# Edge stage opening: one semaphore per tile for the first four record loads, and the loads of super-tiles 1 to 4 each placed behind a gather

## The reference

```python
xs = x[:, :C] @ (W_in2f_s / np.sqrt(C))
xv = jnp.einsum('nci,cf->nfi', x[:, C:].reshape(n, C, 3), W_in2f_v) / np.sqrt(C)
sj = xs[idx_j]
vj = xv[idx_j]
...
h = shifted_softplus(f_ij @ Wf1 + bf1)
W = (h @ Wf2 + bf2) * rcut_ij[:, None]
m_s = s2 * W[:, :2 * F]
m_v = (v2.reshape(e, 2 * F, 3) * W[:, 2 * F:4 * F, None]).reshape(e, 6 * F)
...
agg = jax.ops.segment_sum(x_ij, idx_i, num_segments=n)
```

## Time and profile before

| what | value |
|---|---|
| median of three runs | 1488.72 us |
| profiled execution | 1492.38 us |
| its span | 1490.6 us |
| TensorE busy | 1352.1 us, 91% of the span |
| first record load of the edge stage issued | 442.17 us into the span |
| first gather | 446.04 us |
| last idle time of TensorE for a record load | ends at 463.40 us |
| last gather of the edge stage | 946.0 us |

### The profile page before, as it was taken

How to read it: one execution, slowest core, us unless ns; L and a number is a source line. 1 busy time by engine, 2 the same in 40 slices (tenths; PEclk the granted TensorE clock), 3 DMA queues, 4 the chain that set the end, 5 groups by cost and what they waited for, 6 DMA issues and landing times.

```text
span 1490.6 us, 28549 instructions
## 1 busy us (share of the span) xinstructions
PE 1352.1 (91%) x8675; PEld 610.0 (41%) x8676; DVE 987.0 (66%) x2481; ACT 625.1 (42%) x1097; POOL 753.2 (51%) x772
## 2 busy tenths in 40 slices
PE   6567998778879999999999999875999999999997
PEld 4244444435533333333333333462333343433333
DVE  7846666567737777777777777765564556556554
ACT  5455555554535666666666666571101111111110
POOL 4777777777767666666656666505312211211121
PEclk9667999989889999999999999996999999999999
DMA  5665333333239888888888888572351651524513
GB/s 200 227 216 165 111 115 113 113 115 115 101 111 311 257 257 256 256 256 256 256 248 267 255 257 257 187 282 61 65 192 29 197 183 28 197 82 136 191 29 95
DMA packets 125876, 262.54 MB, mean 176 GB/s; under 512 B 21073, under 2 KB 64808, under 8 KB 125147
## 3 DMA queue, kind: packets, MB, share of 16 engines
q0 software_dynamic: 48416, 141.37, 31.5%
q1 hardware_dynamic: 77410, 120.57, 24.5%
HBM read 204.35 MB, written 63.66 MB: 180 GB/s over the span
## 4 chain that ended last, share of the span: by engine, by line
PE 61%; POOL 22%; issue 8%; DVE 4%; DMA 4%; ACT 1%; SPq 0%; POOLq 0%; DVEq 0%; ACTq 0%
POOL edge_list L456 20%; PE psum L1378 18%; PE psum L1873 17%; PE psum L1885 8%; PE psum L1392 7%; PE psum L1387 5%; PE psum L1371 3%; POOL slot_list L1805 1%; DMA edge_list<-rec,place 1%; DMA out_x<-out_sums 1%; PE psum L1880 1%; DMA shared<-edge_list 1%; DMA slot_list<-pair,slots 1%; PE psum L1491 0%; PE psum L1576 0%
## 5 line engine op out<-in xcount | busy, mean ns | idle before, releaser
L1263 POOL DMA_INDIRECT shared<-node_table,shared x328 | 310.2, 946 | 196.3 <-DVE msg L1344 105.8
L456 POOL DMA_INDIRECT edge_list<-rec,place x313 | 316.9, 1013 | 97.4 <-issue 94.8
L1346 DVE TENSOR_TENSOR msg<-shared,psum 128x768 f32<-128x768 f32 x328 | 310.8, 948 | 0.0
L1378 PE MATMUL psum<-wf,hT 128*32 128x512 f32 x2624 | 298.2, 595 | 1.1 <-ACT hT L1295 0.7
L1873 PE MATMUL psum<-shared,zT 128*64 128x512 f32 (+1 forms) x960 | 295.7, 597 | 1.8 <-DVE zT L1991 1.5
L1301 ACT COPY psum<-bias 128x512 f32<-128x512 f32 x328 | 193.4, 590 | 175.8 <-DVE msg L1346 159.0
L1344 DVE TENSOR_TENSOR msg<-shared,psum 128x256 f32<-128x256 f32 x328 | 136.8, 417 | 120.1 <-PE psum L1378 119.2
L1873 PEld LDWEIGHTS psum<-shared,zT 128*64 128x64 f32 (+1 forms) x960 | 114.5, 159 | 180.7 <-issue 178.6
L1833 POOL DMA_DIRECT2D ids<-slot_list x20 | 11.5, 577 | 291.3 <-DVE zN L1960 266.7
L1885 PE MATMUL psum<-shared,hidT 128*64 128x512 f32 (+1 forms) x480 | 152.8, 597 | 2.8 <-DVE hidT L2012 2.8
L1378 PEld LDWEIGHTS psum<-wf,hT 128*32 128x32 f32 x2624 | 85.1, 110 | 163.4 <-issue 134.1
(11 more groups left out here) (355 smaller groups left out, 1517.8 us busy)
## 6 DMA issues: line engine op xcount, KB each, us to landing
shared<-edge_list SPq DMA_DIRECT2D x332, 130.0 KB
shared<-in_L_ffn_w_gate SPq DMA_DIRECT2D x8, 2048.0 KB, 9.3
shared<-in_L_ffn_w_up SPq DMA_DIRECT2D x8, 2048.0 KB, 14.8
shared<-in_L_ffn_w_down SPq DMA_DIRECT2D x8, 2048.0 KB, 19.6
shared<-node_table,shared POOLq DMA_INDIRECT x328
edge_list<-rec,place POOLq DMA_INDIRECT x313, 2.7
raw<-in_records SPq DMA_DIRECT2D x19, 256.0 KB, 3.8
xrow<-in_x SPq DMA_DIRECT2D x10, 250.0 KB
```

Of the source, the lines that this page charges most:

```text
L456: nc.gpsimd.indirect_dma_start(out=edge_list, out_offset=bass.IndirectOffsetOnAxis(ap=place[:n_, c:c + 1].bitcast(U32), axis=0), in_=rec[: ...
L1263: nc.gpsimd.indirect_dma_start(out=gat[:, k % G, :], out_offset=None, in_=table, in_offset=bass.IndirectOffsetOnAxis(ap=ix, axis=0)).then_ ...
L1346: nc.vector.tensor_tensor(m[:, 1:7, :].rearrange("p (a i) f -> p a i f", a=2), g[:, P:D].rearrange("p (i f) -> p i f", i=3).unsqueeze(1).t ...
L1378: ins = nc.tensor.matmul(WP[k % TS][q * W:(q + 1) * W, :], hT[:, (k // TS) % 2, at:at + W], wf2[:], start=False, stop=True, skip_group_che ...
```

## The change

Four semaphores `first_in[0..3]` are added for the four tiles of super-tile 0. Each of its first loads adds to its own semaphore, and each of the first four gathers waits for its own tile alone. TensorE, before it turns super-tile 0, waits for all four. SP no longer issues the loads of super-tiles 1 and 2 right behind those of super-tile 0: it loads super-tile 1 after gather 0 has landed, super-tile 2 after gather 2, super-tile 3 after gather 4, and super-tile 4 after gather 6.

`records_loaded0` is from now on used only from the second load into slot 0, so that the counts waited for on it are less by one load. The four new semaphores are used again as the first four of `z_out` in the node stage, with 16 more in each count. The number of semaphores stays the same, and so does the data that is moved.

```diff
+                first_in = [sem(f"first_tile{j}_then_z_out{j}") for j in range(TS)]
...
-                        for u in range(3):
-                            fetch(u, ahead[u])
-                        for k in range(LEAD):
-                            sp.wait_ge(gathered[k], 16)
-                        for u in range(3, NU - 1):
-                            fetch(u, ahead[u])
+                        for j in range(TS):
+                            sp.dma_start(er[:, 0, j, :], edge_list[bass.ds(ahead[0][j] * P, P), :]).then_inc(first_in[j], 16)
+                        sp.wait_ge(gathered[0], 16)
+                        fetch(1, ahead[1])
+                        sp.wait_ge(gathered[2], 16)
+                        fetch(2, ahead[2])
+                        sp.wait_ge(gathered[4], 16)
+                        fetch(3, ahead[3])
+                        sp.wait_ge(gathered[6], 16)
+                        fetch(4, ahead[4])
...
                         for k in range(G - 1):
-                            if k % TS == 0:
+                            if k < TS:
+                                pool.wait_ge(first_in[k], 16)
+                            elif k % TS == 0:
                                 pool.wait_ge(rec_in[k // TS], 16 * TS)
                             gather(k)
...
-                            pe.wait_ge(rec_in[u], landed)
+                            if landed is None:
+                                for j in range(TS):
+                                    pe.wait_ge(first_in[j], 16)
+                            else:
+                                pe.wait_ge(rec_in[u], landed)
...
-                        turn_hidden(0, 0, 16 * TS)
+                        turn_hidden(0, 0, None)
...
-                z_out = [z_out] + [sem(f"z_out{i}") for i in range(1, ZB)]
+                z_out = first_in + [z_out]
+
+                def rows_out(u, n_):
+                    return 16 * n_ + (16 if u < TS else 0)
```

More of the change, by code:

```diff
@@ L1273, in gather_ahead @@
                                 if k7 % TS == 0:
-                                    wait_alone(pool, rec_in[(k7 // TS) % NU], it * (16 * TS) + 16 * TS * (1 + k7 // NS))
+                                    u7 = (k7 // TS) % NU
+                                    wait_alone(pool, rec_in[u7], it * (16 * TS) + 16 * TS * ((u7 > 0) + k7 // NS))
                                 wait_alone(pool, made, it * (2 * NS) + (2 * k + 1))
@@ L1426, in super_tiles @@
                                     if u % 2 and (not last or u + d < nu):
-                                        turn_hidden((u + d) % NU, st + d, it * (16 * TS) + 16 * TS * (1 + (u + d) // NU))
+                                        turn_hidden((u + d) % NU, st + d, it * (16 * TS) + 16 * TS * (((u + d) % NU > 0) + (u + d) // NU))
                                 sums(u, st)
@@ L1450, in _ @@
                     for u in range(NU):
-                        wait_alone(sp, rec_in[u], n * (16 * TS) + (16 * TS if u < NU - 1 else 0))
+                        wait_alone(sp, rec_in[u], n * (16 * TS) + (16 * TS if 0 < u < NU - 1 else 0))
                     for k in range(G):
@@ L1557, in _ @@
                         for u in range(ZB):
-                            sp.wait_ge(z_out[u], 16 * len(range(u, NC_, ZB)))
+                            sp.wait_ge(z_out[u], rows_out(u, len(range(u, NC_, ZB))))
                     @block.tensor
@@ L1625, in normalise @@
                             if c >= ZB:
-                                act.wait_ge(z_out[c % ZB], 16 * (c // ZB))
+                                act.wait_ge(z_out[c % ZB], rows_out(c % ZB, c // ZB))
                             nc.scalar.activation(z_at[c % ZB][:CR, :], xrow[:CR, c, :], ACT.Identity, scale=rstd[:CR, c:c + 1],
@@ L1820, in _ @@
                     for u in range(ZB):
-                        pool.wait_ge(z_out[u], 16 * len(range(u, NC_, ZB)))
+                        pool.wait_ge(z_out[u], rows_out(u, len(range(u, NC_, ZB))))
                     pool.wait_ge(ids_found, 1)
```

2 lines of the change are left out of this document (1 added, 1 removed).

## The result

The changed kernel is slower: 1495.53 us in the median of seven runs (1491.63 to 1498.27), against 1489.39 of the kernel before on the same chip (1487.23 to 1496.05); ratio 1.0039, 95% interval 1.0026 to 1.0053. A second series gave 1.0052, 1.0033 to 1.0072. The forecast was 1.5 us more and the result is 5.8 to 7.7 us (the two ratios of 1489): 1495.53 lies above the forecast range of 1488.1 to 1493.2. A loss that can be told had a chance of 22% in the prediction.

The account below looks back on a forecast made before the run. TensorE was taken to bound the edge stage from super-tile 4's turn on; super-tile 2 turned 2.79 us later, less 1.31 us of waits, gives 1.48 us more: 1488.72 becomes 1490.2 us. The range was 1488.1 to 1493.2.

Parts of the forecast that it names:

- A loss that can be told: Whole kernel: slower by more than 0.2%, 3.0 us; chance 22%, against 74% same and 4% faster.
- the 1.31 us of waits comes off if they go: TensorE's waits between the turns of super-tiles 2 and 4 vanish, cutting the 2.79 us delay to 1.48.
- both waits are covered, by TensorE's own lateness: Behind super-tile 2: super-tile 4's loads (0.43 us) and a bank ScalarE seeds (0.39) no longer hold TensorE up.
- super-tile 2 turned 2.79 us later: Opening of the edge stage: TensorE turns super-tile 2 at 454.76 instead of 451.97, its loads now waiting for gather 2.
- The gain for the first gather: Opening: gather 0 waits for one load, not four, and starts 1.62 us earlier, at 444.42; reaches VectorE, not TensorE.
- I take 3.5: Opening: gather 2, started at 446.98, lands in 3.5 us, at 450.48; it took 3.95 before.
- Now only four loads are in front: Reason for gather 2's 3.5 us landing: four loads ahead, in by 445.8, where twelve stood before.
- my 2.4: Opening: super-tile 2's last load lands 2.4 us after issue at 452.32, between 1.99 idle and 3.95 full queue.
- The clock: Rival: TensorE's clock falls in the wait around super-tile 2, costing 1.5 us more, 1491.7, up to 1493.2; chance 13%.
- The third rival: Super-tile 4's loads land late again, taking up to 6.51 us: 4.4 us later in all, 1493.1, or 1492.2; chance 10%.
- The two slower rivals: TensorE's clock falling (13%) and super-tile 4's loads landing late (10%); together 15 of 23 points over 3.0 us.
- three signs of being wrong: Opening: gathers land in under 3 us, the clock falls in its second half, or TensorE waits for super-tile 4's loads.

Follow-up runs that it names:

- two_late: The changed kernel with super-tile 1 loaded at once, super-tile 2 behind gather 2, and 3 and 4 right behind it; ratio 1.0041.
- last_late: The changed kernel with super-tiles 1 and 2 loaded at once, 3 behind gather 2, only 4 behind gather 6; ratio 1.0001.
- tiles_only: The kernel before with only the semaphore per tile for the first four gathers, loads going out as before; ratio 1.0001.
- two_late_filled: two_late with four matmuls that only fill TensorE's wait ahead of the turn of super-tile 2; ratio 1.0039.
- spaced_only: The kernel before with only the spaced loads of super-tiles 1 to 4, the first gather still waiting for all four loads; ratio 1.0055.
- behind_0: The changed kernel with each load group one step earlier: super-tile 1 at once, 2 behind gather 0, 3 behind gather 2, 4 behind gather 4; ratio 1.0024.
- a_again: The changed kernel once more without edit, against the kernel before, with a second profile; ratio 1.0052.
- b_filled: The kernel before with four matmuls that fill TensorE's wait for super-tile 0; ratio 0.9998.
- a_filled: The changed kernel with filling matmuls in TensorE's waits, two ahead of the turn of super-tile 1 and one ahead of super-tile 2; ratio 1.0040.

## Why the prediction was wrong

**The step that failed** is "the 1.31 us of waits comes off if they go", and with it "both waits are covered, by TensorE's own lateness". From the turn of super-tile 2 to that of super-tile 4 TensorE was to lose 1.31 us of waiting; instead that stretch grew by 1.63 us in the mean of three profiles. The step ahead of it, super-tile 2 turned 2.79 us later, was mis-sized: 3.65. The parts follow.

**Place and direction.** Right: the loss is in the opening, TensorE bounds the edge stage from the turn of super-tile 4 on, and the written order makes super-tile 2's loads the dear ones (two_late, last_late). The gain for the first gather was 1.57 us in the first pair of profiles, forecast 1.62, and reached only VectorE and GpSimd (tiles_only).

**Gather 0 and the loads behind it.** Right: the first load of super-tile 1 went out at 5.92, 5.75 and 5.85 us; the forecast 448.14 is 5.97.

**Gather 2.** The step "I take 3.5" was too low: the loads of super-tile 2 went out from 9.40, 9.18 and 9.55 us instead of 8.53. "Now only four loads are in front" overlooked the four of super-tile 1, which the change itself puts beside gather 2, 1.06 us after its start (446.79 and 445.73). The runs bear that out by and large: from its start to 0.22 us ahead of the first load behind it, gather 2 took 4.1 to 4.4 us in the three profiles of the changed kernel, 3.5 to 3.8 in the four of two_late and two_late_filled, where the loads of super-tile 1 were out 1.2 us ahead of it, and 5.2 and 5.3 in last_late and tiles_only, where loads went out until 0.9 us after its start. By the first two some 0.6 us are those four loads, an estimate, since in the three profiles of before gather 2 took 3.6, 4.0 and 4.3 with twelve loads out 0.6 us or more ahead of it. The row of the old gather 2, 3.95, was the nearer one. Cost about 0.85 us. The landing of the last load, 2.56 to 2.78 us for my 2.4, added 0.25. Together the turn of super-tile 2 came at 13.6 in the mean where I had 12.59 (454.76 - 442.17), still inside the bounds of that term (454.1 to 457.2 is 11.9 to 15.0).

**The loads of super-tile 1.** The prediction took 2.4 us for their landing, too. The turn of super-tile 1 came 3.84, 4.62 and 4.07 us after its last load was issued, each time behind a wait for it. Gather 4, which needs these records, so started at 11.54, 12.15 and 11.71 us instead of the forecast 10.23 (452.4 - 442.17), and the last load of super-tile 4 went out at 19.99, 20.96 and 20.18 us, where I had 19.1 at the latest. Both the wait for super-tile 4 and the idle time of TensorE ahead of super-tile 1 hang on this.

**The 1.31 us that "comes off if they go".** Too large, and this was a reading of one profile. From the turn of super-tile 2 to that of 4 the three profiles of before took 11.43, 10.53 and 10.25 us, and the work is 10.12 (0.59 + 9.53). The waits behind super-tile 2 are 1.31, 0.41 and 0.13; I took the worst of three for the rule. The mean is 0.62, so 0.69 us of the slack were not there in most executions. And in the first profile after, where the clock stayed up, one of the waits did not go: 0.61 for the loads of super-tile 4, and 11.01 us in all for the 10.12 of work.

**The clock.** The worst of the chances, and the other large part of the term beside the late loads: 13% for what happened in two of three profiles, in both of two_late, and in those of spaced_only and behind_0. The argument against it, that the idle time is cut in two by the turn of super-tile 1, does not hold: in a_again the clock fell after the first piece alone, 2.44 us, and in the third profile of the changed kernel in the second piece, after 1.44 us idle and 0.66 of work. The price per stretch was too small as well. I took 24 matmul records; the fall covered the 32 of tiles 3 to 6, 5.87 and 6.07 us where the first profile after has 3.64 (the 4.06 and 2.57 that I compared are a row of the timeline and a share of a row of the chain; like for like it is 4.06 and the 2.78 of b_filled). The step from the turn of super-tile 2 to that of 4 grew to 12.94 and 13.14, 1.9 and 2.1 more than in the profile without the fall.

**The sum that the runs give.** Super-tile 2 is turned 3.65 us later (13.61 against 9.96 in the mean of three), and from there to super-tile 4 it takes 1.63 us longer (12.36 against 10.74): 5.3 us, where I had 2.79 - 1.31 = 1.48. Against my 1.48 that is 3.8 us more: 0.86 for the later turn of super-tile 2, 0.69 for slack that was not there, 0.89 for what TensorE lost behind super-tile 2 even with the clock up (11.01 - 10.12), and 1.35 for what the two falls add to that in the mean of three. So the late loads make most of the 5.3 us, and the clock some 1.1 to 1.4 of it: against the two profiles of a_filled (11.50 and 11.29 us from super-tile 2 to 4) it is 1.64 us in each of two executions out of three, 1.1 in the mean.

**The third rival**, super-tile 4's loads late again, is there in the small, 0.61, 1.10 and 0.89 us, in the three profiles in which the loads were spaced as in the change and the clock stayed up (the first of the changed kernel and the two of a_filled), and is hidden where the clock falls. The two slower rivals are alternatives and not a sum. Two of the three signs of being wrong came true: the clock fell, and TensorE waited for the loads of super-tile 4 where it did not fall.

**What stays open.** That the fall costs time was shown in the step in which it lies, by two pairs of profiles; no pair of timed kernels shows it, since 1.5 us is less than the 2 us and more by which their intervals reach to each side. Why the clock falls in one execution of the changed kernel and not in another was not found. Why the landing of the same loads differs by up to 1.7 us between executions of one kernel was not found.

## What to carry to other kernels

Before a load is moved behind another transfer, find the first instruction in program order that needs it on the engine that bounds the stage, and add up transfer, issue and landing with the traffic that the new order itself puts beside them. An earlier start on an engine that isn't the bound was worth nothing here. Where a change opens a new wait of some us on TensorE, count the slower clock of the matmuls behind it as the likely case and not as a rival (here it came in six of seven profiles); and take the slack that is to absorb a delay from several profiles.

## What the runs showed of the hardware

- The clock fell in every profile in or behind the first wait of the edge stage, except in b_filled. There four matmuls stood ahead of super-tile 0, but TensorE had also come late and had hardly a wait, so which of the two kept the clock up is not shown.
- It fell a second time in six of the seven profiles in which super-tile 2 was late and nothing filled the wait (three of the changed kernel, two of two_late, behind_0, spaced_only), and in none of the others. The idle time alone doesn't tell: it fell after 2.44 us in one piece (a_again) and after 1.44, 0.66 of work and part of another 1.55 (the third profile after), but not with 1.84, 0.65 of work and 1.77 (the first profile after), nor with 2.39 and 2.27 in one piece behind filling matmuls (two_late_filled).
- Gather 2, 128 rows of 2 KB with gathers before and behind it, took 3.5 to 4.3 us with no record load started beside it (two_late, two_late_filled, before), 4.1 to 4.4 with four (the changed kernel), and 5.2 to 5.3 with the loads of super-tile 2 still going out at its start (tiles_only, last_late). A record load of 133 KB landed 2.0 us after its issue with an idle queue, and 2.6 to 5.6 with gathers in flight and, at the upper end, further loads behind it.
- A second queue did not bring the first data in sooner (one profile): with eight loads issued by 1.63 us instead of 3.71, the turn of super-tile 0 came 1.9 us later (5.57 against 3.66).
